# Latent attention: fixed bank homes for the score and maximum pairs of a key tile

## The reference, cut to what matters

```python
c_q = h_t @ W_DQ + b_DQ
c_kv = h_t @ W_DKV + b_DKV
...
k_r = (h_t @ W_KR + b_KR)[:, None, :, :]
q = jnp.concatenate([q_c, q_r], axis=-1)
k = jnp.concatenate([k_c, k_r], axis=-1)
scores = jnp.einsum('bhsd,bhtd->bhst', q, k) * scale
attn = jax.nn.softmax(scores, axis=-1)
o = jnp.einsum('bhst,bhtd->bhsd', attn, v_c)
```

## Time and profile before

| | us |
|---|---|
| median of 3 runs | 4268.0 (4266.4 to 4280.18) |
| profiled execution | 4261.15 |
| its span in the trace | 4259.4 |
| TensorE busy | 3541.9 (83%) |
| VectorE busy | 2976.8 (70%) |
| ScalarE busy | 2511.0 (59%) |
| GpSimd busy | 1144.2 (27%) |
| the loop over the heads, first score matmul to last | 1156.9 to 1667.6 |

### The profile page before, as it was taken

How to read it: one execution, slowest core, us unless ns; L and a number is a source line. 1 busy time by engine, 2 the same in 40 slices (tenths; PEclk the granted TensorE clock), 3 DMA queues, 4 the chain that set the end, 5 groups by cost and what they waited for, 6 DMA issues and landing times. The chain is left out here.

```text
span 4259.4 us, 85181 instructions
## 1 busy us (share of the span) xinstructions
PE 3541.9 (83%) x32557; PEld 1588.9 (37%) x32557; DVE 2976.8 (70%) x4355; ACT 2511.0 (59%) x4844; POOL 1144.2 (27%) x1171
## 2 busy tenths in 40 slices
PE   5769998672899998788999997589976689999957
PEld 4623333651222223432222223355646422222237
DVE  6567774557766765668999973437975599999833
ACT  3436666354255555336888884345544468888844
POOL 2610000433086863000000000146864300000016
PEclk7879999786699999878999998799997789999979
DMA  3221110210000000011000000330002210000012
GB/s 124 74 76 40 43 37 22 75 44 9 1 4 4 6 4 18 4 51 33 32 29 24 32 13 2 77 81 4 1 1 79 88 40 32 23 30 31 14 57 74
DMA packets 80791, 152.50 MB, mean 36 GB/s; under 512 B 20852, under 2 KB 47108, under 8 KB 79492
## 3 DMA queue, kind: packets, MB, share of 16 engines
q1 hardware_dynamic: 54768, 105.16, 7.7%
q0 software_dynamic: 12704, 22.97, 1.9%
q10 hardware_dynamic: 12916, 18.93, 1.3%
HBM read 103.76 MB, written 31.20 MB: 32 GB/s over the span
## 5 line engine op out<-in xcount | busy, mean ns | idle before, releaser
L1516 DVE TENSOR_REDUCE 32_heads_mx<-32_heads_mps 128x1 f32<-128x1024 f32 x512 | 602.8, 1220 | 49.6 <-PE 32_heads_mps L1366 47.0
L1516 DVE TENSOR_REDUCE 55_heads_mx<-55_heads_mps 128x1 f32<-128x1024 f32 x512 | 602.8, 1220 | 46.5 <-PE 55_heads_mps L1366 44.0
L1486 ACT ACTIVATE 32_heads_p<-32_heads_sps 128x512 f32<-128x512 f32 x1024 | 553.6, 596 | 86.7 <-PE 32_heads_sps L1392 83.1
L1486 ACT ACTIVATE 55_heads_p<-55_heads_sps 128x512 f32<-128x512 f32 x1024 | 553.6, 596 | 86.0 <-PE 55_heads_sps L1392 82.7
L1516 DVE TENSOR_REDUCE 7_heads_mx<-7_heads_mps 128x1 f32<-128x1024 f32 (+7 forms) x384 | 333.8, 909 | 144.4 <-PE 7_heads_mps L1374 98.8
L2641 DVE TENSOR_REDUCE 21_latent_heads_mx<-21_latent_heads_ring 128x1 f32<-128x1024 f32 x256 | 308.2, 1221 | 130.1 <-PE 21_latent_heads_ring L2473 128.7
L1486 ACT ACTIVATE 7_heads_p<-7_heads_sps 128x512 f32<-128x512 f32 (+3 forms) x640 | 308.1, 534 | 153.0 <-PE 7_heads_sps L1395 113.6
L2608 ACT ACTIVATE 21_latent_heads_p<-21_latent_heads_ring,1_latent_heads_tilt_bias 128x1024 f32<-128x1024 f32 x256 | 271.4, 1110 | 203.9 <-PE 21_latent_heads_ring L2496 197.7
L2417 POOL TENSOR_TENSOR 21_latent_heads_psum<-21_latent_heads_psum,21_latent_heads_p 128x1024 f32<-128x1024 f32 x140 | 323.7, 2359 | 0.0
L1392 PE MATMUL 32_heads_sps<-30_head_rows_qs,30_head_rows_ks 123*32 123x512 bf16 x4096 | 314.4, 383 | 8.5 <-ACT 32_heads_p L1486 5.0
L1392 PE MATMUL 55_heads_sps<-51_head_rows_qs,51_head_rows_ks 123*32 123x512 bf16 x4096 | 314.4, 383 | 8.2 <-ACT 55_heads_p L1486 5.0
(11 more groups left out here) (1216 smaller groups left out, 6694.8 us busy)
## 6 DMA issues: line engine op xcount, KB each, us to landing
3_routed_experts<-in_L0f_experts SPq DMA_DIRECT2D x8, 514.0 KB
9_routed_experts<-in_L0f_experts SPq DMA_DIRECT2D x8, 514.0 KB, 6.8
50_routed_experts<-in_L3f_experts SPq DMA_DIRECT2D x8, 514.0 KB
57_routed_experts<-in_L3f_experts SPq DMA_DIRECT2D x8, 514.0 KB
38_hale_masks_qs<-scratch_q_parts SPq DMA_DIRECT2D x11, 288.0 KB
38_hale_masks_ks<-scratch_k_parts SPq DMA_DIRECT2D x33, 96.0 KB
yT<-scratch_results SPq DMA_DIRECT2D x12, 256.0 KB, 5.4
y<-scratch_results ACTq DMA_DIRECT2D x12, 256.0 KB, 7.0
```

Source lines behind the costliest of these rows:

```text
L1486: act.activation(pslot[x % PS][:, 0:CW - off], sps[e % SB][:, 0:CW - off], ACT.Exp, scale=SCALE / 2).then_inc(ex_done, 1)
L1516: dve.tensor_reduce(mx[h % 2][:, i, half:half + 1], mps[x % 2][:, 0:w], AX.X, ALU.max).then_inc(mx_taken, 1)
```

## The change

The ring is replaced by a table `home` with the bank pair of each pass. In a tile with maxima, with `first` = 0 in even and 1 in odd tiles, s0 has pair `first`, s1 pair 2, m0 pair 1 - `first`, and m1 pair `first` again. Key pairs have pair 2. Tiles without maxima (from tile 11 of head 6 on) keep a ring of three. `wait_for_banks` now waits for the pass that had the same home last.

```diff
--- before.py
+++ after.py
@@ -2380,17 +2380,21 @@
 
         passes = [("keys", 0, 0), ("keys", 0, 1)] + [("max", 0, u) for u in range(4)] + [("keys", 1, 0), ("keys", 1, 1)]
         passes += [("max", 0, u) for u in range(4, U)] + [("max", 1, u) for u in range(AHEAD)]
+        home = [n % RING for n in range(len(passes))]
         for h in range(MLA_H):
-            for p in range(S):
-                passes.append(("score", h, p))
-                if p % 2:
-                    passes += [("max", *unit) for q in (p - 1, p) for unit in maxima_at(h, q)]
-                if h + 2 < MLA_H and p in MAKE:
-                    passes.append(("keys", h + 2, MAKE.index(p)))
+            for j in range(NT):
+                units = maxima_at(h, 2 * j) + maxima_at(h, 2 * j + 1)
+                passes += [("score", h, 2 * j), ("score", h, 2 * j + 1)] + [("max", *unit) for unit in units]
+                first = j % 2
+                home += [first, 2, 1 - first, first] if units else [(2 * j) % RING, (2 * j + 1) % RING]
+                if h + 2 < MLA_H and 2 * j + 1 in MAKE:
+                    passes.append(("keys", h + 2, MAKE.index(2 * j + 1)))
+                    home.append(2)
         place = {which: n for n, which in enumerate(passes)}
+        previous = [max((m for m in range(n) if home[m] == home[n]), default=None) for n in range(len(passes))]
 
         def pair_of(which):
-            return ring[place[which] % RING]
+            return ring[home[place[which]]]
 
         def bank(which, x):
             return pair_of(which)[:, x * CW:(x + 1) * CW]
@@ -2401,8 +2405,8 @@
         assert sorted(freed) == list(range(len(passes)))
 
         def wait_for_banks(pe, which):
-            if place[which] >= RING:
-                pe.wait_ge(*freed[place[which] - RING])
+            if previous[place[which]] is not None:
+                pe.wait_ge(*freed[previous[place[which]]])
 
         def half_of(pair):
             return slice(2 * CW * pair, 2 * CW * (pair + 1))
```

## The result

| | before | after |
|---|---|---|
| median of 7 runs | 4266.4 (4261.3 to 4280.18) | 4294.44 (4289.79 to 4298.06) |
| profiled execution, its span | 4261.15, 4259.4 | 4298.06, 4296.3 |
| first exponential of the loop to the last | 510.0 | 544.0 |

The ratio is 1.0064 (95% interval 1.0052 to 1.0076): 27 us slower. The forecast was 4283, with 4266 to 4296 as range; it had the direction and half of the size. In the profiled executions 34.0 of the 36.9 us between the spans lie in the loop over the heads; 2.9 lie outside it, just under the 3 that the prediction names as a sign of being wrong.

What follows compares the result with a forecast made beforehand. TensorE was taken as busiest but not saturated, with scores waiting for exponentials in plain tiles. Key places 15.6, less 2.0 for plain tiles, plus 1.5 for the clock, on 4268.0 gave 4283, range 4266 to 4296.

Steps and rivals of the forecast that it cites:

- the 3 that the prediction names as a sign of being wrong: Outside the changed stage: a change of more than 3 us there would show the prediction wrong.
- Where the waits go: Tiles with maxima: s0' waits for maximum m0, s1' for exp s1, or for the subtraction behind keys; no instruction moves.
- The key step, 1.30 x 12 = 15.6: At 12 places behind keys in heads 0 to 5, the late s1' costs 1.30 us each, 15.6 slower.
- The plain part, -2.0: Plain tiles, net of a late maximum in tile 11: 0.33 us saved a head, 2.0 over heads 0 to 5.
- head of 69.4 at full clock: Sign of being right: a head takes 69.4 us at full clock (67.1 + 2.6 - 0.3).
- the sum of steps, 13.6: Key places and plain part over heads 0 to 5: 15.6 - 2.0 = 13.6 us slower, without the clock.
- The clock, +1.5: Behind keys: one more stretch at 1.2 GHz than the four before, costing 1.5 us.
- Rival B: The clock falls at every key place, twelve stretches of 1.5 us; 4294, chance 0.17.

Runs made afterwards that it cites:

- e12: The changed kernel with m0' put in front of the late s1' in TensorE's order behind keys; 4289.77, ratio 1.0045.
- e3: The changed kernel with the f32 matmuls of s0' behind keys made three times in all, the extra results overwritten; 4269.00, ratio 1.0011.
- e8: The kernel before, ring of three unchanged, with the f32 matmuls of s1' behind keys made three times in all; 4256.53, ratio 0.9972.
- e5: The changed kernel with four extra matmuls on row groups 2 and 3 behind s0' after a key pair; 4286.91, ratio 1.0051.
- e7: The changed kernel with the f32 matmuls of s0' behind keys made one more time; 4285.21, ratio 1.0040.
- e6: The changed kernel with four extra matmuls on row groups 0 and 1, ahead of the late s1' to run beside it; 4289.50, ratio 1.0048.

## Why the prediction was half right

**Where the waits go: right.** No instruction moved, s0 and s1 changed their waits, and s1' came 0.05 behind the subtraction at each of the 12 key places.

**The key step, 1.30 x 12 = 15.6: right.** It is 1.28 at full clock, nearly the 1.27 from the late s1' to m0'. e12 shows what the queue has to do with it: with m0' no longer behind s1' it falls by 0.53, m0's own step; the other 0.75 stays.

**The plain part, -2.0: nearly right.** Tiles 1 to 3 run at 3.46, 3.47 and 3.53 from exponential to exponential where 3.58 stood, but the gain is 0.28 a head and not 0.33, 1.7 in all. The prediction's head of 69.4 at full clock is 69.38 in e3, and the sum of steps, 13.6, is 13.65 between e8 and e3.

**The clock, +1.5: this is the step that failed.** I wrote "After the change the gap is as long" and took one stretch more. In the profiled executions the clock costs 26.3 us after (442.47 - 416.17) and 6.1 before (408.58 - 402.52): +20 instead of +1.5. What the runs show against it: the pause is longer, not as long, 25.2 us in 12 places against 22.1, since the pair s1', which had covered its start, now comes behind it. Ten places fall and not five; how much of that is due to the longer pause, to the half-filled array or to the moment is open (e5 to e7, e12). And a fall is not 3.4 but often 6.8 us long, since the late s1' now runs in it, at half speed and on half of the array; e6, with a full array there, has seven short ones and one long. Rival B had the falls, and I gave it 0.17, but I priced one at 1.5, where one place in the changed kernel cost 2.84 (6.18 - 3.34).

Over many runs the clock's share is less than in the traces: 27 - 13.65 leaves 13 to 14 instead of 1.5. By the ratios the clock costs 23 us after (1.0064 against 1.0011 in e3) and 12 before (e8, between 8 and 16 by its interval), so the usual run of before loses more than its profiled one. That 4294 lies inside the range of 4266 to 4296 is owed to rival B's place in it, not to the forecast's own sum.

**The rule beside rival B.** The Trainium skill (TensorE: Matmul & The Clock Gate, "A second HAM failure mode: psum-queue depth-cycling") tells of pauses between matmul groups that make the clock go back and forth. The traces of the changed kernel agree in this: 0.50 for 6.8 us behind a pause of 2.10, then full clock again, at ten of 12 places, though not at all, as case B had it. The page puts the cost between the bursts; here the trace shows it in the matmuls, s1' taking 2.03 us instead of 1.13.

## What to carry to other kernels

A bank that is freed late should go to the consumer that stands last in the engine's queue, since everything behind the waiting instruction waits with it; here moving it one pass forward cost 1.28 us a time. Look at what a pause of the matmul engine does to the clock, and not only at its length: unfilled pauses of 1.25 to 2.10 us let it fall at 4 to 10 of 12 places, and what works right behind the pause went with how long a fall lasts. One trace is not enough to count falls by, as e12's times in two groups show. Where such a pause can't be removed, fill it, best with work that is needed anyway (the product first).

## What I had not expected of the hardware

- Matmuls on two of the four row groups, repeated through the gap, kept the clock up wholly in e3's trace (no fall in 12 places, 0.39 us idle); with 1.25 us idle left there were six falls (e7).
- A fall in the changed kernel lasted 6.8 us at seven of ten places, in the kernel before always 3.4; with all row groups at work behind the pause seven of eight were short (e6).
- The same pause of 1.57 us in the same order of work gave falls in heads 0 to 2 and none in heads 3 to 5 (e12).
- Repeating matmuls three times into the same bank in 12 places made the kernel 0.28% faster (e8).
